# Attention sums divided untransposed by groups of eight heads, score maxima made further ahead

## The chip, the cores and the metric

One core of a Trainium2 chip runs the whole program. The metric is the device time of one execution in microseconds (us); lower is better.

## The reference, cut to what matters

A block of a transformer in float32: cross and self attention with 16 heads of 16 channels, then a mixture of experts.

```python
# x: (4, 512, 256), ctx: (4, 1601, 128)
def block(x, ctx):
    h = layernorm(x)
    q, k, v = heads(h @ Wq + bq), heads(h @ Wk + bk), heads(h @ Wv + bv)
    y = softmax(causal(q @ k.T * 0.25)) @ v
    qc, kc, vc = heads(h @ Wcq + bcq), heads(ctx @ Wck + bck), heads(ctx @ Wcv + bcv)
    y = y + softmax(qc @ kc.T * 0.25) @ vc
    x = x + tanh(g[0]) * (merge(y) @ Wp + bp)
    h = layernorm(x)
    return x + tanh(g[1]) * (shared_expert(h) + top2_of_7_experts(h))
```

## The kernel before, in words

There are 64 units of attention (4 sequences by 16 heads), called heads here. The program has three stages. The first prepares the queries, keys and values of all heads; it splits them into three bfloat16 parts and stores them in the device memory (`q_parts`, `k_parts`). The second is a loop over heads. The third projects the attention's result, normalizes again, and runs the shared expert, the router and the routed experts.

**The loop over heads.** A softmax needs the maximum of each query's scores before the exponentials. TensorE therefore makes the scores twice: first untransposed in 16 *pieces* a head (`MAX_PIECES`: twelve of 512 columns for the cross scores, then `tail`, `pair`, `self2`, `self3`), which VectorE reduces to maxima (`reduce_bank`, L1242); then transposed, in eight *groups* (`GROUPS`), with the maxima subtracted through two more rows of the operands. ScalarE takes the exponential of each group (L993), GpSimd masks the diagonal tiles (L1144), and TensorE multiplies them with the values in four phases (`values`, L669). The values have a column of ones, so that a phase also gives the sum of the exponentials.

**The maxima run ahead.** In the step of head u, the pieces c = 0 to 7 are the last eight of head u+1, and c = 8 to 15 are the first eight of head u+2 (`HALF` = 8, `reduce_piece`, `max_piece`). After its piece c = 7 VectorE joins the maxima in three small operations (`max_parts`, L1254, L1257, L1260). TensorE then transposes the result (`max_rows`, L592) after c = 11, ScalarE copies it out (L953), and a transfer on SyncE's queue puts it in its rows (`rows_load`, L471), for which the first scores of the next head wait.

**The order on TensorE is written out** by `schedule`: for each group g the piece 2g, the scores of g, the piece 2g+1, and then for odd g something more: the last phase of values of the head before (g = 1), the first phase and `norm` (g = 3), `rows` and the second phase (g = 5), the third phase (g = 7). Each engine runs its own instructions in order and waits on semaphores.

**The three banks.** The sixteen pieces, `norm` and `rows` (`ENTRIES`, 18 of them) take three PSUM banks in turn (`bank_of`, `RING` = 3). An entry may start when the entry three places before it in this order has been read out (`bank_free`):

```python
at = ENTRIES.index(item)
before = ENTRIES[at - RING]
```

**The division.** After the last phase ScalarE copies the sums of the head before (`sums_out`, L974), 128 rows by 512 queries. TensorE transposes them in four products (`norm`, L718), ScalarE copies the result (`norm_out`, L982), GpSimd adds the three cross parts (`cross_sums`, L1133, L1135), VectorE takes the reciprocals (L1326), and GpSimd multiplies and adds (`head_output`, L1125, L1128).

**After the loop** TensorE turns the attention's output back, 32 transposes with a copy by ScalarE for every four (L540, L1015), and projects it tile by tile (`project`, 16 tiles, L760). VectorE adds each tile to x (L1382) and normalizes it (`tail_stats`, `tail_scale`). `turn_xn(0)` transposes the first normalized sequence before the last four tiles, and the shared expert follows (`shared_up`, L786; ScalarE's `shared_silu`, L1032; VectorE's `shared_hidden`, L1352).

Of the kernel before, what the change touches and what calls it, by code (L numbers as in the profile page):

```python
# [17 lines left out]
NB = 4  # L18
# [74 lines left out]
HALF = NMAX // 2  # L93
MAXED = NMAX + HALF
# [4 lines left out]
def schedule():  # L99

    out = []
    for g in range(NG):
# [15 lines left out]
ENTRIES = [item for item in PE_ORDER if item[0] in ("max", "norm", "rows")]  # L118
# [6 lines left out]
RSUM_AT = HALF + 4  # L125

def run_steps(eng, step):

    step(0, 0, False, True, True)  # L130
    step(1, 1, True, True, True)
    heads = NR
    turns = (NU - 2 - 2) // heads
    with eng.Fori(0, turns) as i:
        for h in range(heads):
            step(i * heads + (h + 2), (h + 2) % NR, True, True, True)
    for u in range(heads * turns + 2, NU):
        step(u, u % NR, True, u + 1 < NU, u + 2 < NU)
# [13 lines left out]
def program(nc, a):  # L152
    ctx = ExitStack()
    with ctx:
# [10 lines left out]

        xn_rows = nc.dram_tensor("xn_rows", (NTOK, C), F32, kind="Internal").ap()
# [7 lines left out]
        xnT = sb("xnT", [P, 2, B * T])  # L174
# [42 lines left out]
        last_at = place["wq"][0]  # L217
        assert last_at + KSIZE + QSIZE <= place["wv"][0]
        kst = [region("kst")[:, r * KSIZE:(r + 1) * KSIZE] for r in range(NR - 1)]
        qst = [region("qst")[:, r * QSIZE:(r + 1) * QSIZE] for r in range(NR - 1)]  # L220
        kst.append(arena[:, last_at:last_at + KSIZE])
        qst.append(arena[:, last_at + KSIZE:last_at + KSIZE + QSIZE])
# [9 lines left out]
        rsum = sb("rsum", [P, TT, 2])  # L232
        yb = sb("yb", [P, TT, 2, D])

        router = sb("router", [P, 4 * NT * E8])
        sums = router[:, 0:TT * 4 * (D + 1)].rearrange("p (t q d) -> p t q d", t=TT, q=4)
        lg, key, s1, s2 = [router[:, NT * E8 * i:NT * E8 * (i + 1)].rearrange("p (t e) -> p t e", t=NT)
                        for i in range(4)]
        wr_cols = yb.rearrange("p a b d -> p (a b d)")[:, 0:2 * VW].rearrange("p (k w) -> p k w", k=2)
# [15 lines left out]
        def rt(*shape):  # L255
# [7 lines left out]
            if len(shape) == 3:  # L263
# [47 lines left out]
                 "m_all m_hi m_split rows_tr rows_evac rows_ready masked o_evac norm_mm norm_evac sums_half sums_in rsum_ready y_parts y_done  dve_chain "  # L311
                 "pool_chain y_turned y_freed proj_mm xn_turned xn_freed x2_ready tanh_done bias_gated x_biased wr_ready logits_mm logits_out logits_turned gap_ready exp2_done "
# [88 lines left out]
        def res_slot(s):  # L401
# [4 lines left out]
            return xnT[:, s % NS - NB, b * T:(b + 1) * T]  # L406
# [32 lines left out]
        def _(sp):  # L439
# [28 lines left out]
            def rows_load(v, r):  # L468

                sp.wait_ge(S["rows_evac"], v + 1)  # L470
# [39 lines left out]
            for v in range(NU - 2, NU):  # L510
                rows_load(v, v % NR)
# [1105 lines left out]
```

## Time and profile before

| what | value |
|---|---|
| median of 3 runs | 1414.95 us (1414.21 to 1415.78) |
| the profiled execution | 1413.27 us, of which the span from its first to its last instruction is 1411.5 us |
| TensorE busy | 1368.6 us, 97% of the span |
| VectorE, ScalarE, GpSimd busy | 880.9, 727.3, 365.4 us |
| preparation, loop over heads, the rest | up to 132.6 us, to 922.8 us, to the end |

The profile counts a matrix product as busy from its start to the end of its drain, so that two products that follow each other overlap; short waits hide in that overlap and have to be read from the starts in the timeline.

### The profile page before, as it was taken

To read this page: it belongs to the slowest core of one execution; us is meant where nothing else is said; L and a number is where in the kernel's file an instruction comes from. 1 tells how busy PE (TensorE), PEld (TensorE's weight loads), DVE (VectorE), ACT (ScalarE), POOL (GpSimd) and SP (SyncE) were. 2 spreads that over 40 slices of the span, in tenths; PEclk is the share of its full clock that TensorE was granted. 3 is DMA by queue.
4 is the path that set the end of the run, shared out by engine and by line. 5 is a ranking of instruction groups with operands and counts; after the bars stand their busy time and mean duration, and the time that the engine had idled before them with its cause. 6 is when DMAs were issued, how large, how long until landed. Compare 5 with 4: busy or idle time off the path is not lost.

```text
span 1411.5 us, 27301 instructions
## 1 busy us (share of the span) xinstructions
PE 1368.6 (97%) x7688; PEld 694.0 (49%) x7689; DVE 880.9 (62%) x1804; ACT 727.3 (52%) x1107; POOL 365.4 (26%) x743
## 2 busy tenths in 40 slices
PE   7988999999999999999999999989999999999997
PEld 4544333333333333333333333364556777777775
DVE  6776888888888888888888888653532222222221
ACT  4644667677777676767676767732210222222221
POOL 5655222222222222222222222200001232233232
PEclk9999999999999999999999999999999999999999
DMA  8754111111111111111111111057004122112111
GB/s 246 237 186 154 43 53 51 48 50 48 47 49 50 51 50 50 49 48 48 48 51 51 50 49 50 7 218 297 0 1 134 26 33 34 30 30 37 30 30 23
DMA packets 57711, 98.43 MB, mean 70 GB/s; under 512 B 7441, under 2 KB 42001, under 8 KB 56657
## 3 DMA queue, kind: packets, MB, share of 16 engines
q1 hardware_dynamic: 50384, 88.10, 18.8%
q0 software_dynamic: 7296, 9.97, 4.5%
q8 instruction: 15, 0.25, 0.1%
q14 instruction: 16, 0.12, 0.0%
HBM read 69.20 MB, written 28.58 MB: 69 GB/s over the span
## 4 chain that ended last, share of the span: by engine, by line
PE 88%; DMA 2%; DVE 2%; ACT 1%; issue 1%; POOL 1%; SPq 0%; POOLq 0%; ACTq 0%; DVEq 0%
PE ps L669 19%; PE ps L834 13%; PE ps L651 13%; PE ps L551 13%; PE ps L847 7%; PE ps L786 5%; PE ps L797 3%; PE ps L718 3%; PE ps L654 2%; PE ps L565 2%; PE ps L858 2%; DMA k_parts<-work 2%; PE ps L555 1%; PE ps L592 1%; PE ps L625 1%
## 5 line engine op out<-in xcount | busy, mean ns | idle before, releaser
L1242 DVE TENSOR_REDUCE mx<-ps 128x1 f32<-128x512 f32 (+1 forms) x832 | 515.1, 662 | 99.6 <-PE ps L551 69.3
L993 ACT ACTIVATE arena<-ps 128x1024 f32<-128x1024 f32 (+1 forms) x512 | 484.3, 995 | 138.7 <-PE ps L651 135.2
L669 PE MATMUL ps<-arena 128*32 128x512 f32 (+5 forms) x2432 | 290.9, 525 | 0.6 <-ACT arena L993 0.4
L551 PE MATMUL ps<-arena 96*128 96x512 bf16 x768 | 263.0, 382 | 7.3 <-DMA arena<-k_parts 2.9
L651 PE MATMUL ps<-arena 98*128 98x512 bf16 x832 | 264.4, 381 | 5.0 <-DMA arena<-rowst 4.9
L1144 POOL TENSOR_SCALAR_AFFINE_SELECT arena<-arena 128x128 f32<-128x128 f32 x256 | 74.8, 292 | 439.2 <-ACT arena L993 429.3
L834 PE MATMUL ps<-arena,work 128*128 x608 | 186.4, 460 | 0.6 <-issue 0.6
L551 PEld LDWEIGHTS ps<-arena 96*128 96x128 bf16 x768 | 74.1, 96 | 178.0 <-DVE mx L1242 103.2
L1520 DVE TENSOR_TENSOR work<-work,ps 128x352 f32<-128x352 f32 x76 | 39.6, 521 | 179.1 <-ACT work L1061 179.1
L834 PEld LDWEIGHTS ps<-arena,work 128*128 128x128 f32 x608 | 112.5, 190 | 57.4 <-issue 1.1
L1242 DVE TENSOR_REDUCE mneg<-ps 128x2 f32<-128x512 f32 (+2 forms) x192 | 112.4, 640 | 23.9 <-PE ps L561 23.4
L1061 ACT ACTIVATE work<-ps 128x352 f32<-128x352 f32 x76 | 35.2, 463 | 164.6 <-PE ps L834 164.6
L1186 POOL DMA_INDIRECT out<-bv,slot_table x38 | 59.9, 1575 | 207.3 <-DVE bv L1526 197.5
L669 PEld LDWEIGHTS ps<-arena 128*32 128x32 f32 (+1 forms) x2432 | 56.6, 108 | 113.1 <-issue 110.5
L651 PEld LDWEIGHTS ps<-arena 98*128 98x128 bf16 x832 | 76.5, 98 | 66.2 <-DMA arena<-rowst 6.1
L847 PE MATMUL ps<-arena,work 128*128 (+1 forms) x456 | 105.0, 379 | 0.8 <-ACT work L1067 0.8
L847 PEld LDWEIGHTS ps<-arena,work 128*128 128x128 f32 (+1 forms) x456 | 83.6, 190 | 11.4 <-issue 1.1
L1176 POOL DMA_INDIRECT wp<-xn_rows,slot_table x38 | 37.7, 993 | 173.5 <-DVE slot_table L1509 137.7
L1066 ACT ACTIVATE work<-ps 128x256 f32<-128x256 f32 x76 | 29.0, 382 | 99.7 <-PE ps L858 99.6
L786 PE MATMUL ps<-xnT,arena 128*128 128x512 f32 x176 | 77.1, 595 | 0.4 <-DVE work L1352 0.4
L654 PE MATMUL ps<-arena 98*128 98x512 bf16 (+3 forms) x256 | 66.1, 299 | 0.0
L1526 DVE TENSOR_SCALAR bv<-ps,router 128x256 f32<-128x256 f32 x38 | 18.4, 484 | 64.1 <-PE ps L847 64.1
(161 smaller groups left out, 1406.8 us busy)
## 6 DMA issues: line engine op xcount, KB each, us to landing
arena<-in_experts SPq DMA_DIRECT2D x8, 2176.0 KB, 12.2
arena<-k_parts SPq DMA_DIRECT2D x64, 198.1 KB
arena<-k_parts SPq DMA_DIRECT2D x64, 132.1 KB
arena<-q_parts SPq DMA_DIRECT2D x64, 96.0 KB
k_parts<-work SPq DMA_DIRECT2D x16, 300.0 KB, 5.2
q_parts<-work SPq DMA_DIRECT2D x12, 384.0 KB, 5.4
arena<-k_parts SPq DMA_DIRECT2D x64, 66.0 KB
arena<-q_parts SPq DMA_DIRECT2D x64, 64.0 KB
```

Of the source, the lines that this page charges most:

```text
L551: mm = pe.matmul(out, qx[:, qt * P:(qt + 1) * P], ks[0:KROWS, T + j * CHUNK:T + (j + 1) * CHUNK], start=True, stop=True)
L651: mm = pe.matmul(bk[:, 0:w], kst[r][0:KROWS + MROWS, T + kt * P:T + (kt + 1) * P], qst[r][0:KROWS + MROWS, 1, :], start=True, stop=True)
L654: mm = pe.matmul(bk[:, o0:o0 + w], kst[r][0:KROWS + MROWS, kt * P:(kt + 1) * P], qst[r][0:KROWS + MROWS, 0, kt * P:T], start=True, stop=True)
L669: mm = pe.matmul(ps[32 * q:32 * q + VW, 6, b0:b1], vst[0:kn, r % VR, TT + kt if cross else kt, :], pr[0:kn, c0:c0 + b1 - b0], start=(phase ...
L718: mm = pe.transpose(out[:, t * P:(t + 1) * P], osb[:, t * P:(t + 1) * P], ident[:, :])
L786: mm = pe.matmul(ps[:, 2 * (k0 % 2) + j, :], wgus[:, k, w0:w0 + P], xnT[:, k, tb * T:(tb + 1) * T], start=(k == 0), stop=(k == 1))
L834: mm = pe.matmul(ps[:, 2 * c + j, 0:CH], xgT[:, b, k, :], weights[:, bass.ds(e, 1), o:o + CH], start=(k == 0), stop=(k == 1))
L847: mm = pe.matmul(ps[:, 4, 0:C], hidT[0:m, it, :], weights[0:m, bass.ds(e, 1), o:o + C], start=(it == 0), stop=(it == IT - 1))
L993: act.activation(pr[:, c0:c0 + n], ps[:, 2 * (g % 2):2 * (g % 2) + 2, :].rearrange("p b n -> p (b n)")[:, 0:n], ACT.Exp, scale=SCALE).then ...
L1144: pool.affine_select(out=exps, in_=exps, pattern=[[1, P]], compare_op=ALU.is_ge, fill=0.0, base=0, channel_multiplier=-1).then_inc(S["mask ...
L1186: pool.indirect_dma_start(out=a["out"], out_offset=bass.IndirectOffsetOnAxis(slot_table[:, i, 1:2], 0), in_=yt[:, i % 2, :], in_offset=Non ...
L1242: return dve.tensor_reduce(m, out, AX_X, ALU.max)
```

## The change

- The division isn't transposed any more. Each head's sums are stored in the device memory (`o_parts`). For a group of eight heads they are loaded back so that 128 partitions are eight heads by 16 channels, the form that the projection reads. The denominators are loaded with their queries spread over partitions, summed by GpSimd and inverted by VectorE, stored and loaded again as broadcast rows; GpSimd sums, multiplies and adds tiles of 128x512. These steps are spread over the heads h = 2 to 7 of the next group.
- `norm` becomes the entry `spare`, which runs nothing, and `norm_out` is gone. `rows` moves from g = 5 to g = 3, ahead of the first phase of values. `HALF` = 8 becomes `BACK` = 5: c = 0 to 4 are the last five pieces of head u+1, and 27 pieces instead of 24 are made in the preparation.
- The transfer of the maxima's rows is issued by ScalarE, behind a wait for its own copy.
- The fourth operand buffer lies in `shared`; the shared expert's weights are loaded four heads before the end of the loop.
- After the loop there are no transposes of the output. The projection of sequences 2 and 3 is mixed with the first products of the shared expert, and the last group's division runs meanwhile. The loads of the routed experts come after the stores of the normalized rows.

```diff
-HALF = NMAX // 2
-MAXED = NMAX + HALF
+BACK = 5
+DONE = NMAX - BACK
+MAXED = NMAX + DONE
...
         if g == 3:
-            out += [("values", 0), ("norm",)]
+            out += [("rows",), ("values", 0)]
         if g == 5:
-            out += [("rows",), ("values", 1)]
+            out += [("spare",), ("values", 1)]
...
             def bank_free(u, *item):
                 at = ENTRIES.index(item)
-                before = ENTRIES[at - RING]
-                step = u if at >= RING else u - 1
+                at -= RING if ENTRIES[at - RING][0] != "spare" else 2 * RING
+                before = ENTRIES[at]
+                step = u if at >= 0 else u - 1
...
-                v, piece = (u + 1, c + HALF) if c < HALF else (u + 2, c - HALF)
+                v, piece = (u + 1, c + DONE) if c < BACK else (u + 2, c - BACK)
                 reduce_bank(v, piece, bank_of("max", c)).then_inc(S["max_red"], 1)
...
                 for c in range(NMAX):
-                    if (c < HALF and nxt) or (c >= HALF and nxt2):
+                    if (c < BACK and nxt) or (c >= BACK and nxt2):
                         reduce_piece(u, c)
-                    if nxt and c == HALF - 1:
+                    if nxt and c == BACK - 1:
                         for i in range(3):
                             max_parts(u + 1, i)
-                    if prev and c == RSUM_AT:
-                        reciprocals(u)
+                    if h == RECIP_IN and c == RECIP_AT:
+                        reciprocals(group)
...
                 act.activation(rowst[:, :], out[0:MROWS * 2 * TT, 0:P], ACT.Copy).then_inc(S["rows_evac"], 1)
+                act.wait_ge(S["rows_evac"], v + 1)
+                act.dma_start(qst[r][KROWS:KROWS + MROWS, :, :].rearrange("p i t -> p (i t)"), rowst[:, :]
+                              ).then_inc(S["rows_ready"], 16)
...
+            def head(u, j=None, h=None, loads=True):
+                sp.wait_ge(S["qk_done"], u * NG + NG)
+                if loads:
+                    stack_loads(u + NR, (BEGUN + h if j is not None else u) % NR)
+                if h == 2:
+                    den_load(j)
+                    num_load(j, 0)
+                if h == 3:
+                    num_load(j, 1)
+                if h == 4:
+                    num_load(j, 2)
+                    num_load(j, 3)
+                if h == 5:
+                    recip_load(j)
+                sums_store(u)
+                if h == 3:
+                    recip_store(j)
...
-            for b in range(B):
-                if b == B - 1:
-                    turn_xn(0)
-                project(b)
+            project(0)
+            project(1)
+            turn_xn(0)
             pe.wait_ge(S["shared_load"], 16)
-            shared_up(0)
+            shared_up(0, 0, 1)
+            project(2)
+            shared_up(0, 1, 2)
+            project(3)
+            shared_up(0, 2, IT)
...
             deviations(2 + B, 1, 2)
             xn_out(0)
+            shared_silu(0, 0, 1)
             deviations(3 + B, 2, 3)
+            shared_silu(0, 1, 2)
             deviations(4 + B, 3, 4)
-            shared_silu(0)
+            shared_silu(0, 2, IT)
...
-            shared_hidden(0)
+            second_norm(0, 2 * TT)
+            shared_hidden(0, 0, 1)
+            second_norm(2 * TT, 3 * TT)
+            shared_hidden(0, 1, 2)
+            second_norm(3 * TT, NT)
+            shared_hidden(0, 2, IT)
```

On VectorE `second_norm` runs the same operations per tile as before (`residual`, `tail_stats`, `tail_scale`), with the last group's reciprocals after tile 5. On ScalarE the store of the first normalized sequence stands ahead of `deviations(2 + B)` and behind a wait for the scaled rows.

## Rows read from the trace of the kernel before

**Rows 1.** The page, its first part: busy time, share, instructions.
```profile
PE 1368.6 (97%) x7688; PEld 694.0 (49%) x7689; DVE 880.9 (62%) x1804; ACT 727.3 (52%) x1107; POOL 365.4 (26%) x743
```
**Rows 2.** Windows: stretch, length, busy PE, PEld, DVE, ACT, POOL, clock, DMA share, GB/s.
```profile
400.00:800.00 400.00, 398.90 (x2743) 153.48 (x2737) 335.96 (x652) 283.34 (x360) 95.83 (x294) 1.00 0.15 50
```
**Rows 3.** Timeline of PE, one head: start, length (us), engine, line, what, count.
```profile
888.84 0.39 PE L551 MATMUL ps<-arena 96*128 96x512 bf16 x1
...
891.96 0.30 PE L555 MATMUL ps<-arena 96*128 96x65 bf16 x4
...
893.83 1.07 PE L669 MATMUL ps<-arena 128*32 128x512 f32 x8
894.83 0.66 PE L718 MATMUL ps<-ident,work 128*128 128x128 f32 x4
895.32 0.38 PE L551 MATMUL ps<-arena 96*128 96x512 bf16 x1
...
896.79 0.38 PE L551 MATMUL ps<-arena 96*128 96x512 bf16 x1
897.22 0.22 PE L592 MATMUL ps<-identb,mparts 128*16 128x128 bf16 x1
897.33 1.06 PE L669 MATMUL ps<-arena 128*32 128x512 f32 x8
...
899.85 0.38 PE L551 MATMUL ps<-arena 96*128 96x512 bf16 x1
900.16 1.06 PE L669 MATMUL ps<-arena 128*32 128x512 f32 x8
901.15 0.39 PE L551 MATMUL ps<-arena 96*128 96x512 bf16 x1
```
**Rows 4.** Timeline of DVE in the same head.
```profile
893.06 1.75 DVE L1242 TENSOR_REDUCE mneg<-ps 128x2 f32<-128x512 f32 x3 [0.34 <-PE ps L561]
894.85 0.17 DVE L1254 TENSOR_REDUCE mneg<-mx 128x4 f32<-128x16 f32 x1
...
895.26 0.17 DVE L1260 SCALAR_TENSOR_TENSOR mparts<-mneg,mparts 128x8 bf16<-128x8 f32 x1
895.74 2.54 DVE L1242 TENSOR_REDUCE mx<-ps 128x1 f32<-128x512 f32 x4 [0.31 <-PE ps L551]
```
**Rows 5.** Timeline of ACT in that head; of SP, an issue.
```profile
896.17 1.83 ACT L993 ACTIVATE arena<-ps 128x1024 f32<-128x1024 f32 x2 [0.26 <-PE ps L651]
897.89 0.25 ACT L953 ACTIVATE rowst<-ps 16x128 bf16<-16x128 f32 x1
...
505.11 0.68 SPq L471 DMA_DIRECT2D arena<-rowst  x1
```
**Rows 6.** Timeline where the loop starts: PE, ACT, SP.
```profile
132.59 0.39 PE L551 MATMUL ps<-arena 96*128 96x512 bf16 x1 [1.89 <-DVE arena L1315]
137.54 1.03 PE L651 MATMUL ps<-arena 98*128 98x512 bf16 x2 [4.56 <-DMA arena<-rowst]
...
138.67 1.28 ACT L993 ACT_TABLE_LOAD   x1 [6.41 <-PE ps L651]
139.97 1.94 ACT L993 ACTIVATE arena<-ps 128x1024 f32<-128x1024 f32 x2
...
128.40 2.93 SPq L490 DMA_DIRECT2D k_parts<-arena  x2
```
**Rows 7.** Timeline behind the loop: PE, DVE.
```profile
921.51 1.35 PE L669 MATMUL ps<-arena 128*32 128x512 f32 x14 [0.42 <-ACT arena L993]
...
932.03 10.87 PE L760 MATMUL ps<-wp,xnT 128*128 128x256 f32 x48
...
970.10 3.60 PE L786 MATMUL ps<-xnT,arena 128*128 128x512 f32 x8
...
933.18 0.48 DVE L1382 SCALAR_TENSOR_TENSOR x<-ps,tg,x 128x256 f32<-128x256 f32 x1 [6.01 <-PE ps L760]
...
942.57 0.40 DVE L1224 TENSOR_SCALAR shared<-x,mv,rs 128x256 f32<-128x256 f32 x1
```

More of the change, by code:

```diff
@@ L117 @@
 PE_ORDER = schedule()
-ENTRIES = [item for item in PE_ORDER if item[0] in ("max", "norm", "rows")]
+ENTRIES = [item for item in PE_ORDER if item[0] in ("max", "spare", "rows")]
 RING = 3
@@ L124 @@
 SCALE_LAG = 5
-RSUM_AT = HALF + 4
-def run_steps(eng, step):
[L130 to L137, printed above, removed]
+GH = P // D
+NGRP = NU // GH
+BEGUN = GH - 2
+TURNS = NGRP - 1
+DENS_IN, RECIP_IN, SUMS_IN, OUT_IN, RECIP_AT = 3, 4, 6, 7, 3
+assert GH % NR == 0 and BEGUN >= 2
+def run_steps(eng, step):
+    for u in range(BEGUN):
+        step(u, u % NR, u > 0, True, True)
+    with eng.Fori(0, TURNS) as i:
+        for h in range(GH):
+            step(i * GH + (BEGUN + h), (BEGUN + h) % NR, True, True, True, i, h)
+    for u in range(GH * TURNS + BEGUN, NU):
         step(u, u % NR, True, u + 1 < NU, u + 2 < NU)
@@ new lines, in _ @@
+            for u in range(BEGUN):
+                head(u)
+            with sp.Fori(0, TURNS - 1) as i:
+                for h in range(GH):
+                    head(i * GH + (BEGUN + h), i, h)
+            for h in range(GH):
+                u = (TURNS - 1) * GH + BEGUN + h
+                head(u, TURNS - 1, h, u + NR < NU)
+                if u == NU - NR:
+                    sp.dma_start(weights[:, SHARED, :], a["experts"][SHARED]).then_inc(S["shared_load"], 16)
+            den_load(NGRP - 1, 0, GH - 2)
@@ L577, in bank_free @@
                         pe.wait_ge(S["max_red"], min(n, NU * NMAX - MAXED) if isinstance(n, int) else n)
-                elif before[0] == "norm" and not (isinstance(u, int) and u == 0):
-                    pe.wait_ge(S["norm_evac"], step)
                 elif before[0] == "rows":
@@ L723, in _ @@
             values(NU - 1, (NU - 1) % NR, NPH - 1)
-            norm(NU)
             def logits():
@@ L973, in sums_out, with step @@
                 act.wait_ge(S["pv_done"], u * NPH)
+                if not (isinstance(u, int) and u == 1):
+                    act.wait_ge(S["o_written"], u * 16 - 16)
                 act.activation(osb[:, :], ps[:, 6, :], ACT.Copy).then_inc(S["o_evac"], 1)
[L976 to L984 removed]
+            def step(u, r, prev, nxt, nxt2, group=None, h=None):
                 for g in range(NG):
@@ L1378, in tail_scale, with residual @@
                 scale_rows(t)
-            for t in range(NT):
+            def residual(t):
                 dve.wait_ge(S["proj_mm"], t + 1)
```

265 lines of the change are left out of this document (146 added, 119 removed).

## The prediction

> **What bounds the kernel now.** I read the page first: TensorE is busy 97% of the span, VectorE 62%, ScalarE 52% [rows 1]. Then the windows of the loop over heads: in 400 us TensorE is busy 398.9, VectorE 336, ScalarE 283 [rows 2], at a granted clock of 1.00 (2.4 GHz). So the loop goes at TensorE's pace, and work taken from TensorE should be gained in full, unless a wait takes its place. VectorE, at 84%, is the engine to watch. Third, the timeline of one head, by starts, since the overlap of products hides short waits [rows 3]. A head takes 901.15 - 888.84 = 12.31 us. Fourth, the two ends of the loop [rows 6, 7].
>
> **What is removed.** The four transposes of `norm` take 895.32 - 894.83 = 0.49 us a head [rows 3]. The small waits around `rows` can be seen too: from the 512-column piece at 896.79 to the values at 897.33 are 0.54 us, where the same pair of steps without `rows` takes 900.16 - 899.85 = 0.31 [rows 3]. When `rows` leaves that place, 0.23 us go: the product itself (0.11) and its wait for a bank. Naively a head would take 12.31 - 0.49 - 0.23 + 0.11 = 11.70 us, and 61 full heads 37 us less.
>
> **Where a new wait comes.** `rows` now stands at g = 3, at index 8 of the ring, and needs the bank of entry 5, which is the piece c = 5. `BACK` = 5 puts the three operations of `max_parts` on VectorE between the reductions of c = 4 and c = 5. The piece c = 4 is the first product after the last values phase, so that VectorE has run dry by then. I count from that restart of TensorE, t0, in the trace 891.96 [rows 3].
> - TensorE, without a wait: the pieces from c = 4 to c = 7 have the same columns as before within 4 of some 2,200, so the values phase could start at +1.87 (893.83 - 891.96 [rows 3]), and `rows`, 0.11 long, goes ahead of it at about +1.75.
> - VectorE: c = 4 is `self3`, a product of 512 columns and one of 128. The second starts at +0.22, is 0.22 long like L592 [rows 3], and a reduction starts 0.04 behind a product's end (895.32 + 0.38 against 895.74 [rows 3, 4]). So its reduction starts at +0.48. A 512-wide one takes 0.69 with 0.62 between starts (four in 2.54 [rows 4]); it ends at +1.16. `max_parts` goes from 0.04 behind that (893.06 + 1.75 against 894.85) to 895.26 + 0.17, that is 0.62 behind it: +1.78 [rows 4]. The reduction of c = 5 starts at +1.71 to +1.78, since a start may overlap the last operation's end, and ends at +2.40 to +2.47.
> - TensorE's `rows` starts 0.17 behind that: in the old place the second of the four reductions ends at 895.74 + 0.62 + 0.69 = 897.05, and `rows` starts at 897.22 [rows 3, 4]. So it starts at +2.57 to +2.64, not +1.75, and the values at +2.68 to +2.75 instead of +1.87.
>
> Sum of a head: +0.81 to +0.88 for values that start late, -0.49 for the transposes, -0.23 around the old place of `rows`, and 0.04 that I allow for the changed order of the short pieces: **+0.13 to +0.20 us a head, I take 0.15**. Steps 1 to 61, 61 heads: **+9.2 us** (8 to 12). Behind the values phase VectorE is later than before, and I checked the ring on: the piece c = 11 needs the reduction of c = 8, which ends at +4.8, and comes at +5.15.
>
> **What lies beside other work.** In each step nothing on the other engines reaches TensorE's next need.
> - ScalarE loses `norm_out`, and copies the rows at about +2.83, 0.25 long, to +3.08 [rows 5]. Its new transfer has no row on this engine; SyncE's issue of the same transfer took 0.68 us [rows 5]. I take that: ScalarE is free at +3.8. The next exponential is wanted at +3.68 + 0.85 = +4.53 (896.17 - 895.32 is the 0.85 [rows 3, 5]). Cover 0.7 us; bounds 0.1 and 1.5 us for the issue, the upper price is a rival below.
> - SyncE gets per head one store of 256 KB, and per group four loads of denominators, four of numerators, two stores and two broadcast loads, each at 0.4 to 0.8 us of issue, as its present ones. With six stack loads that is at most some 9 us in a head of 12.4. Each load is wanted a head or more after its issue. The mean rate, 50 GB/s [rows 2], not quite doubles.
> - GpSimd does two to three 128x512 operations at the end of steps h = 6 and h = 7. I bound each by 0.3 and 1.6 us; the mask of the next head is wanted some 5 us later. If it were late, the values would be.
>
> **The start of the loop.** TensorE stands 4.56 us for the rows' transfer, which SyncE issues behind the last stores [rows 6]. ScalarE now issues it much earlier. What is late next: the exponentials, for ScalarE waits for the last `k_parts` store from the arena, whose issue begins near 130.8 [rows 6]. With a landing of 3.6 us, as these stores take, that is 134.5; then the table load of 1.28 us, and the first exponential starts near 136 instead of 139.97 [rows 6]. Less waiting at the low clock adds a little. I take -4.9 us (-3 to -6.5). The three further pieces in the preparation cost 0.22 us each on TensorE or 0.62 on VectorE, where nothing hides them: +1.0 (0.2 to 2). Together **-3.9**.
>
> **The last two heads** are at ScalarE's pace, without maxima of later heads. They lose one copy each: **-0.6** (0 to -1.5).
>
> **Behind the loop.** The last values end at 922.8. The first projection starts at 932.03, and the second sequence's products of the shared expert at 970.10 [rows 7]. So before it was 9.2 + 38.1 = 47.3 us, and in the 38.1 TensorE hardly waits. Now the projection starts at once, but `turn_xn(0)` comes after 8 tiles, at 8 x 0.906 = 7.25 us (10.87 / 12 [rows 7]). Its rows depend on VectorE: from the first residual to the scaling of the fourth tile are 942.57 - 933.18 = 9.4 us [rows 7]. One residual less and the reciprocals more, it is done at 1.15 + 9.25 + 0.4 = 10.8, and TensorE stands 3.7 us, then 1.1 more until ScalarE, which has a transfer to issue first, has copied. The last group's division needs three round trips of transfers, which I put at 17 us; it is wanted at 23. Two more waits of up to 1 us hang on ScalarE, which alternates between square root and Silu and so loads tables four times more, at 1.28 us each [rows 6]. In the sum 42 to 44 us instead of 47.3: **-4.3** (-2 to -6.5).
>
> In this trace a table load of 1.28 us is followed by its activation 0.02 us later [rows 6]. The Trainium skill (ScalarE: Activation LUTs, What ACT_TABLE_LOAD costs) gives 2.66 us for a switch, a drain of 1.38 included. By that rule the two switches on TensorE's path would cost 2.8 us more, an estimate from that page, and the tail would gain 1.5 us; I keep the row.
>
> **Sum.** +9.2 - 3.9 - 0.6 - 4.3 = +0.4 us on the profiled execution of 1413.3, that is 1413.7; its median of runs lies 1.7 us higher, so **1415.3 us**. About 0.2% (2.8 us) is what a measurement of this kernel can tell from no change.
>
> **The rivals.**
> - *The wait for the bank doesn't bind (faster).* If VectorE reduces c = 5 early, only `max_parts` remains: `rows` at +1.95, the values at +2.06, and a head is 0.19 - 0.49 - 0.23 + 0.04 = -0.49 us. 61 heads give -30, with the ends 1376 us. For it: the waits of today's ring are at most 0.2 us. Against it: VectorE's order in the code, and that the same wait shows at 897.22. Half of it gives 1395. Chance 0.18.
> - *ScalarE's own transfer holds the exponentials (slower).* Place: behind the copy of the rows, ahead of group 4. It decides from an issue, with the wait for its copy, of over 1.45 us; twice SyncE's 0.68 is 1.36. At 1.85 it would cost 0.4 us a head, +24, 1440 us. For it: the wait for its own copy has no row. Against it: the issue's row. Chance 0.10.
> - *The transfers come late (slower).* The broadcast loads and small rows fill the queue, and SyncE is late with the stacks or a store that ScalarE waits for. One late head in eight by 1.5 us is +12, 1427 us. Chance 0.06.
> - *The change doesn't bring its start and its tail.* The rows' transfer isn't what holds the start, since the stores are, and the tail waits eat its gain: +8, 1423 us. That lies in the forecast's own range.
>
> **How the numbers follow.** The forecast's mechanism has 0.66, with its own range from 1407 to 1424; within it I give 0.18 to a gain above 0.2%, 0.27 to neither, 0.21 to a loss, since the head's +0.15 may be off by 0.1 (6 us). With the rivals: faster 0.36, same 0.27, slower 0.37. The range reaches half way into the first rival and takes in the late transfers: 1396 to 1427; it leaves out the full first rival (about 0.10) and ScalarE's (0.10).
>
> **What would show it.** In the profile after, L592 starts about 0.8 us later than the piece before it would let it, with the reduction of c = 5 ending 0.17 us earlier; VectorE's three small operations stand between two 512-wide reductions; a head takes 12.4 to 12.5 us; the exponentials start near 136; TensorE idles some 4 to 5 us about 7 us behind the loop. It is wrong if a head takes under 12.2 or over 12.7 us, or if the release of L592 or L669 is ScalarE or a transfer.

## The result and the profile after

The changed kernel took 1432.48 us in the median of 4 runs (1429.79 to 1434.69); the kernel before took 1414.58 beside it (4 runs, 1412.98 to 1415.78). The ratio is 1.0126, with an interval from 1.0106 to 1.0147: **slower by 1.3%**, where 1415.3 was predicted and 1396 to 1427 was the range. The profiled execution took 1434.69 us, with a span of 1433.0.

The page's first part of the changed kernel, and its windows for the stretch of [rows 2], for the tail, and for a stretch of the shared expert:

```profile
PE 1347.3 (94%) x7400; PEld 664.3 (46%) x7401; DVE 881.6 (62%) x1748; ACT 709.4 (50%) x1039; POOL 332.8 (23%) x543
```
```profile
400.00:800.00 400.00, 373.23 (x2513) 132.78 (x2509) 323.28 (x602) 264.40 (x315) 74.34 (x184) 1.00 0.26 84
...
944.00:988.00 44.00, 38.06 (x133) 23.84 (x132) 26.22 (x79) 15.17 (x23) 6.79 (x7) 0.92 0.44 145
1068.00:1108.00 40.00, 37.98 (x147) 25.59 (x145) 7.12 (x17) 2.08 (x5) 3.10 (x3) 0.91 0.32 105
```

Against [rows 1] TensorE has 21 us less work, and in the loop it is busy 373.2 us of 400 instead of 398.9 [rows 2]: it lost work, and stands for some 27 us of these 400. The clock in the loop stayed at 1.00, so the clock has no part in it there.

Where the time went, by the starts of TensorE's steps in both profiled executions:

| stretch | before | after | difference | predicted |
|---|---|---|---|---|
| up to the start of step 1 | 151.94 | 147.13 | -4.8 | -3.9 |
| steps 1 to 61 | 749.21 | 774.59 | **+25.4** | +9.2 |
| steps 62, 63 | 21.64 | 20.63 | -1.0 | -0.6 |
| loop's end to the second sequence's shared products | 47.3 | 45.8 | -1.5 | -4.3 |
| the rest | 441.4 | 444.9 | +3.5 | 0 |

**One head.** The timeline of TensorE in the changed kernel, in the columns of [rows 3]; 504.23 is the restart t0 behind the last values phase, L663 is `max_rows`, L740 the values:

```profile
501.08 0.39 PE L623 MATMUL ps<-arena 96*128 96x512 bf16 x1
...
504.23 0.39 PE L637 MATMUL ps<-arena 96*128 96x512 bf16 x1
...
505.76 0.38 PE L623 MATMUL ps<-shared 96*128 96x512 bf16 x1
506.83 0.22 PE L663 MATMUL ps<-identb,mparts 128*16 128x128 bf16 x1 [0.69 <-DVE mx L1317]
507.05 1.06 PE L740 MATMUL ps<-arena 128*32 128x512 f32 x8
...
513.66 0.39 PE L623 MATMUL ps<-shared 96*128 96x512 bf16 x1
...
516.55 0.34 PE L637 MATMUL ps<-shared 96*128 96x384 bf16 x1 [1.18 <-DVE mx L1317]
```

VectorE in the same head and the next:

```profile
501.50 1.03 DVE L1317 TENSOR_REDUCE mx<-ps 128x1 f32<-128x512 f32 x2 [0.29 <-PE ps L623]
...
504.71 0.69 DVE L1317 TENSOR_REDUCE mneg<-ps 128x1 f32<-128x512 f32 x1 [1.10 <-PE ps L638]
505.44 0.17 DVE L1329 TENSOR_REDUCE mneg<-mx 128x4 f32<-128x16 f32 x1
...
506.01 1.89 DVE L1317 TENSOR_REDUCE mx<-ps 128x1 f32<-128x512 f32 x3
...
515.80 1.03 DVE L1317 TENSOR_REDUCE mx<-ps 128x1 f32<-128x512 f32 x2 [2.00 <-PE ps L633]
```

What is to be seen: the reduction of c = 4 starts at t0 + 0.48 and `max_rows` at t0 + 2.60, as the walk of the prediction had them, and `max_rows` is released by VectorE. A head takes 513.66 - 501.08 = 12.58 us. The second stand, at 516.55, was not foreseen. It comes once in eight heads, six times in the loop: such a head takes 13.90 to 14.14 us. In the VectorE rows it is a wait of 2.00 us ahead of the reduction at 515.80. In the head before, the same reduction, at 501.50, waits 0.29 us for its piece, an L623.
**ScalarE in that head:**

```profile
507.17 0.27 ACT L1009 ACTIVATE rowst<-ps 16x128 bf16<-16x128 f32 x1 [0.19 <-PE ps L663]
507.46 0.62 ACTq L1011 DMA_DIRECT2D arena<-rowst  x1
508.91 1.83 ACT L1046 ACTIVATE arena<-ps 128x1024 f32<-128x1024 f32 x2 [1.48 <-PE ps L722]
```

Its own transfer costs 0.62 us and is over 0.8 us before the next exponential, which waits for TensorE.

**The tail.** TensorE, then VectorE and GpSimd in the same stretch:

```profile
942.35 7.17 PE L815 MATMUL ps<-wp,xnT 128*128 128x256 f32 x32
954.69 1.97 PE L612 MATMUL ps<-ident,shared 128*128 128x128 f32 x8 [5.16 <-DVE shared L1299]
957.44 5.70 PE L839 MATMUL ps<-xnT,arena 128*128 128x512 f32 x8 [0.78 <-ACT xnT L1070]
962.97 3.62 PE L815 MATMUL ps<-wp,xnT 128*128 128x256 f32 x16
966.42 3.60 PE L839 MATMUL ps<-xnT,arena 128*128 128x512 f32 x8
```
```profile
948.24 1.14 DVE L1296 TENSOR_SCALAR sd<-mv 128x4 f32<-128x4 f32 x1
...
950.84 0.54 DVE L1399 RECIPROCAL work<-work 128x64 f32<-128x64 f32 x1
...
954.15 0.17 DVE L1296 TENSOR_SCALAR sd<-mv 128x4 f32<-128x4 f32 x1
```
```profile
948.09 1.27 POOL L1189 TENSOR_TENSOR xnT<-xnT,shared 128x512 f32<-128x512 f32 x1 [0.50 <-DMA work<-work]
949.50 1.26 POOL L1192 TENSOR_TENSOR xnT<-xnT,shared 128x512 f32<-128x512 f32 x1
```

TensorE stands 5.16 us for the fourth scaled tile, and after that stand the same eight products take 5.70 us instead of 3.60. The same small VectorE operation takes 0.17 us alone and 1.14 beside a GpSimd operation, where it ends 0.02 us behind that operation's end.

**The rest.** The row after, in the changed kernel, of the down products that begin the last part of the shared expert:

```profile
1093.34 9.32 PE L850 MATMUL ps<-arena,shared 128*128 128x256 f32 x24 [1.75 <-DVE x L1525]
```

In the kernel before the same 24 products, after the same wait of 1.75 us, took 6.03. They took 6.03 in all eleven later profiles, of changed kernels too. So this +3.3 us belongs to this one execution: the window around it has a granted clock of 0.91. It also accounts for the profiled execution lying 2.2 us above its median.

### The profile page after: what moved, and what is told of

Its sections match the earlier page's. It is cut to its first block, busy times and chain, and to the rows that moved or that the text cites. A ratio compares the mean times of both kernels' runs of the same rounds, so it can differ in the third digit from the quotient of the medians.

```text
span 1433.0 us, 26072 instructions
## 1 busy us (share of the span) xinstructions
PE 1347.3 (94%) x7400; PEld 664.3 (46%) x7401; DVE 881.6 (62%) x1748; ACT 709.4 (50%) x1039; POOL 332.8 (23%) x543
## 4 chain that ended last, share of the span: by engine, by line
PE 80%; DVE 9%; issue 3%; DMA 1%; ACT 1%; POOL 0%; DVEq 0%; POOLq 0%; SPq 0%; ACTq 0%
PE ps L740 19%; PE ps L887 13%; PE ps L623 10%; PE ps L722 10%; PE ps L900 7%; PE ps L839 5%; PE ps L850 4%; DVE mx L1317 3%; DVE mneg L1317 3%; PE ps L637 2%; PE ps L911 2%; PE ps L725 2%; PE ps L696 1%; PE ps L663 1%; PE ps L815 1%
## 5 line engine op out<-in xcount | busy, mean ns | idle before, releaser
L740 PE MATMUL ps<-arena 128*32 128x512 f32 (+5 forms) x2432 | 290.9, 525 | 1.4 <-ACT arena L1046 0.6
L623 PE MATMUL ps<-arena 96*128 96x512 bf16 x576 | 198.1, 382 | 4.4 <-DMA arena<-k_parts 2.5
L722 PE MATMUL ps<-arena 98*128 98x512 bf16 x624 | 197.9, 380 | 1.5 <-ACT arena L1046 1.4
L1317 DVE TENSOR_REDUCE mneg<-ps 128x2 f32<-128x512 f32 (+2 forms) x192 | 118.4, 642 | 63.0 <-PE ps L638 63.0
L623 PEld LDWEIGHTS ps<-arena 96*128 96x128 bf16 x576 | 55.6, 97 | 169.4 <-DVE mx L1317 116.6
L740 PEld LDWEIGHTS ps<-arena 128*32 128x32 f32 (+1 forms) x2432 | 56.7, 108 | 106.9 <-issue 98.6
L722 PEld LDWEIGHTS ps<-arena 98*128 98x128 bf16 x624 | 59.0, 98 | 50.3 <-ACT arena L1046 4.3
L722 PE MATMUL ps<-shared 98*128 98x512 bf16 x208 | 65.5, 379 | 0.0
L623 PE MATMUL ps<-shared 96*128 96x512 bf16 x192 | 65.5, 381 | 0.0
```

Source lines behind the costliest of these rows:

```text
L623: mm = pe.matmul(out, qx[:, qt * P:(qt + 1) * P], ks[0:KROWS, T + j * CHUNK:T + (j + 1) * CHUNK], start=True, stop=True)
L722: mm = pe.matmul(bk[:, 0:w], kst[r][0:KROWS + MROWS, T + kt * P:T + (kt + 1) * P], qst[r][0:KROWS + MROWS, 1, :], start=True, stop=True)
L740: mm = pe.matmul(ps[32 * q:32 * q + VW, 6, b0:b1], vst[0:kn, r % VR, TT + kt if cross else kt, :], pr[0:kn, c0:c0 + b1 - b0], start=(phase ...
L1317: return dve.tensor_reduce(m, out, AX_X, ALU.max)
```

## The experiments

Theories at the outset. **Main:** the loop is lengthened by a ring wait that the place of `max_parts` (`BACK` = 5) makes, 0.27 us a head, and by a stand of VectorE at its jump back. **Rivals:** the long loop bodies as such; the transfers; GpSimd's larger tiles, which fall in the same steps as the jump.

### Four pieces behind instead of five

```diff
-BACK = 5
+BACK = 4
```

> The changed kernel with BACK = 4, nothing else: the three operations of max_parts then run on VectorE during the last phase of values, one piece earlier. Theory (the rows' bank is held by the piece c = 5, whose reduction stands behind max_parts): L592's successor L663 starts at about +1.93 us from the restart of TensorE instead of +2.60, a head in the loop takes 11.8 to 11.95 us instead of 12.58, and the whole 40 to 46 us less than the changed kernel, 1387 to 1392 us. Rival (the new transfers and GpSimd's tiles slow the loop, the wait only shows it): a head stays above 12.4 us and the whole above 1425 us.

Measured: 1392.71 us (1391.13 to 1394.98), ratio 0.986 (0.9844 to 0.9877). The same places of one head, of TensorE and VectorE:

```profile
487.83 0.38 PE L623 MATMUL ps<-shared 96*128 96x512 bf16 x1
488.26 0.22 PE L663 MATMUL ps<-identb,mparts 128*16 128x128 bf16 x1
488.48 1.06 PE L740 MATMUL ps<-arena 128*32 128x512 f32 x8
```
```profile
486.04 0.17 DVE L1329 TENSOR_REDUCE mneg<-mx 128x4 f32<-128x16 f32 x1
...
486.79 2.54 DVE L1317 TENSOR_REDUCE mx<-ps 128x1 f32<-128x512 f32 x4 [0.17 <-PE ps L623]
```

`max_parts` now stands ahead of the piece c = 4, in time in which VectorE waits anyway, and TensorE's `rows` hardly waits any more: it comes 0.43 us after the piece instead of 1.07. A head takes 11.94 us, 0.64 less. So the wait was the whole difference between this kernel and one that is 1.4% faster than before. The heads at the jump still take 13.2 to 13.5 us.

### The rows at their old place

Eight pieces behind, and `rows` with ScalarE's copy at g = 5, so that the untransposed division stands almost alone:

```diff
-BACK = 5
+BACK = 8
-            out += [("rows",), ("values", 0)]
+            out += [("spare",), ("values", 0)]
-            out += [("spare",), ("values", 1)]
+            out += [("rows",), ("values", 1)]
```

> The changed kernel with BACK = 8 and the rows' entry back at g = 5 (spare at g = 3): only the new division, with ScalarE's transfer of the rows. Theory (the moved maxima cost, the division gains): a head takes 12.31 - 0.49 + 0.13 = 11.95 us, since the wait for the bank of c = 9 stays, the whole 36 to 42 us less than the changed kernel, 1391 to 1397 us. If the rows' transfer now lands too late for the next head's first scores, L722 waits for DMA arena<-rowst, and the head is 12.0 to 12.6 us. Rival (the division's transfers and GpSimd's tiles cost): above 1420 us with no such wait.

Measured: 1421.33 us (1420.05 to 1426.2), ratio 1.0065 (1.004 to 1.009). Many heads take 11.76 to 11.94 us, but almost a third take 12.8 to 14.1, among them the six at VectorE's jump with 13.3 to 13.5, and three, which are not at the jump, 15.5 to 15.7; the mean of steps 1 to 61 is 12.54. ScalarE's issue and TensorE's next use of the rows:

```profile
476.68 0.62 ACTq L1011 DMA_DIRECT2D arena<-rowst  x1
```
```profile
481.42 0.60 PE L722 MATMUL ps<-arena 98*128 98x512 bf16 x2 [1.27 <-DMA arena<-rowst]
...
494.39 0.60 PE L722 MATMUL ps<-arena 98*128 98x512 bf16 x2 [0.86 <-DMA arena<-rowst]
```

From the issue to the use are 4.7 us, for 4 KB. So the small transfer lands late here, while 256 KB transfers are under way, and TensorE waits for it 17 times, 21.3 us in all. These waits, the jumps and what follows them make 0.60 us a head over 11.94, more than the 0.49 of the saved transposes. That the large transfers make it late fits, but no run took them away. The second half of the change, the rows two groups sooner, is what the first half needs. It was the number of pieces that was chosen wrongly with it.

### Loop bodies of eight heads in the kernel before

```diff
-    heads = NR
+    heads = 2 * NR
```

> The kernel before with a loop body of eight heads instead of four on TensorE, VectorE, ScalarE and GpSimd; the work is the same. Theory (VectorE stands at the jump back because a body of eight heads has to be fetched again): VectorE stands some 2 us at each of the 7 jumps, TensorE 1.0 to 1.4 us, and the whole is 7 to 10 us slower than before, 1422 to 1425 us. Rival (GpSimd's three tiles of 128x512 at the end of the step h = 7 hold VectorE): no such stand, within 2 us of before.

Measured: 1412.10 us (10 runs, 1411.16 to 1414.1), ratio 0.9996 (0.9986 to 1.0006). No head takes more than 12.40 us. The DMA view shows no packet of the queue q14, instructions, between 300 and 800 us, where the changed kernel has 25:

```profile
q14 instruction: 25, 0.20, 0.1%
```

A body of eight heads alone is not what makes VectorE stand: from its branch to the next instruction are 0.3 us here and in the kernel before, against 2.8 to 3.0 in the changed kernel.

### VectorE's jump at another place of the head

VectorE's loop is turned, so that its body begins ahead of c = 4 of one step and ends there in another; GpSimd's tiles stay where they were.

```diff
-            run_steps(dve, step)
+            CUT = 4
...
+            step(BEGUN, BEGUN % NR, True, True, True, c1=CUT)
+            with dve.Fori(0, TURNS) as i:
+                for h in range(GH):
+                    step(i * GH + (BEGUN + h), (BEGUN + h) % NR, True, True, True, i, h, c0=CUT)
+                    step(i * GH + (BEGUN + h + 1), (BEGUN + h + 1) % NR, True, True, True, i, h + 1, c1=CUT)
```

> The changed kernel, with VectorE's jump back moved from ahead of the piece c = 0 to ahead of c = 4, where VectorE stands 1.1 us in each head anyway; the order of its work is the same. Theory (the jump's fetch): the step of 13.93 us in eight becomes 13.2 to 13.6, since 1.1 of some 2 us are covered but what is left delays the rows directly, and the whole is 2 to 5 us faster than the changed kernel. Rival (GpSimd's tiles): the stand of 2 us before the piece c = 0 stays where it is, and the time too.

Measured: 1438.28 us (1434.68 to 1440.08), ratio 1.0173 (1.015 to 1.0195). That the kernel would gain was a miss; where the stand is was not:

```profile
521.22 0.69 DVE L1317 TENSOR_REDUCE mneg<-ps 128x1 f32<-128x512 f32 x1 [2.63 <-PE ps L623]
```

The stand moved with the jump, from the pieces 14 and 15 to the piece c = 4, where TensorE has less work ahead of it to hide a stand; the six heads at the jump take 14.0 to 16.9 us. GpSimd's tiles are thereby out.

### VectorE's heads written out

```diff
-            run_steps(dve, step)
+            for u in range(NU):
+                j, h = divmod(u - BEGUN, GH) if BEGUN <= u < GH * TURNS + BEGUN else (None, None)
+                step(u, u % NR, u > 0, u + 1 < NU, u + 2 < NU, j, h)
```

> The changed kernel with VectorE's part of the 64 heads written out without a loop; the work and its order are the same, the other engines keep their loops. Theory (the stand of 2 us in every eighth head belongs to VectorE's own jump back): the steps of 13.9 us disappear, 7 x 1.35 = 9 us, and where VectorE waits on constants instead of registers the steps are 12.45 to 12.58, so 9 to 17 us less than the changed kernel, 1416 to 1424 us. Rival (another engine's jump or a transfer at that place holds VectorE): the stand stays and the time is within 3 us.

Measured: 1418.03 us (8 runs, 1416.31 to 1418.55), ratio 1.0031 (1.0021 to 1.0042), 14.5 us under the changed kernel. No long head is left, and the others take 12.50 instead of 12.58. The stands were 1.32 to 1.56 us over a normal head, six times, 8.4 us. The 0.08 a head is 4.5 us over the 56 heads of the loop. The third part, of 1.6 us, is within what runs differ by. The 0.08 shows between the piece c = 7 and the values, 1.20 us here and 1.29 in the changed kernel.

### TensorE's waits ahead of the rows

The values behind `rows` wait for the values' load (`v_ready`) and for ScalarE's last copy (`o_evac`). In the changed kernel they start 0.22 us behind `rows`, which itself needs 0.11. Both waits are put ahead of `rows`:

```diff
-                        if item[1] == 0:
-                            pe.wait_ge(S["v_ready"], u + 1)
-                            if prev:
-                                pe.wait_ge(S["o_evac"], u)
                         values(u, r, item[1])
-                    elif item[0] == "rows" and nxt:
+                    elif item[0] == "rows":
+                        pe.wait_ge(S["v_ready"], u + 1)
+                        if prev:
+                            pe.wait_ge(S["o_evac"], u)
+                        if not nxt:
+                            continue
```

> The changed kernel with TensorE's waits for v_ready and o_evac put ahead of the rows instead of behind them. Theory (behind a late L663 TensorE works off four waits before the values, which is why they start 0.22 us after it instead of 0.11): the values start 0.11 to 0.17 us after L663, a head takes 12.47 to 12.53 instead of 12.58 us, and the whole is 3 to 7 us faster than the changed kernel. Rival (the gap comes from the weights' load): no change.

Measured: 1425.63 us (1423.18 to 1427.0), ratio 1.0087 (1.007 to 1.0103), 6.9 under the changed kernel:

```profile
504.02 0.22 PE L663 MATMUL ps<-identb,mparts 128*16 128x128 bf16 x1 [0.70 <-DVE mx L1318]
504.13 1.07 PE L740 MATMUL ps<-arena 128*32 128x512 f32 x8
```

The distance is 0.11 now, and a head of the loop takes 12.48 us. Between `rows` and the values the trace of the changed kernel has two instructions that wait or compute registers, and this one has one: what had long been reached still costs 0.11 us behind an instruction that is late.

Steps 1 to 5 lie ahead of the loop and are written out in every version. There the same edit has the opposite effect: 12.53 us a head against 12.41 in the changed kernel. The changed kernel, then this one:

```profile
177.55 0.22 PE L663 MATMUL ps<-identb,mparts 128*16 128x128 bf16 x1 [0.53 <-DVE mx L1317]
177.76 1.06 PE L740 MATMUL ps<-arena 128*32 128x512 f32 x8
```
```profile
177.02 0.22 PE L663 MATMUL ps<-identb,mparts 128*16 128x128 bf16 x1 [0.74 <-DVE mx L1318]
177.14 1.07 PE L740 MATMUL ps<-arena 128*32 128x512 f32 x8
```

In both `rows` waits for VectorE's reduction. It starts 0.04 us behind VectorE's signal in the first and 0.25 in the second. So the edit helps in the loop and harms in written-out heads; "The same with the waits ahead" comes back to it.

### The first turn later in the tail

`turn_xn(0)` behind the twelfth tile instead of the eighth; ScalarE's and VectorE's orders go with it.

```diff
             project(0)
             project(1)
+            project(2)
             turn_xn(0)
             pe.wait_ge(S["shared_load"], 16)
-            shared_up(0, 0, 1)
-            project(2)
-            shared_up(0, 1, 2)
+            shared_up(0, 0, 2)
             project(3)
```

> The changed kernel with the third sequence's projection ahead of the first transposes of the normalized rows and of the shared expert. Theory (TensorE stands 5.2 us ahead of these transposes, and falls to the low clock): the 3.6 us of projection go into that stand and the products behind it run at 2.4 GHz, 4 to 7 us faster than the changed kernel. Rival (VectorE sets the pace there, which then only starts the shared expert later): within 2 us.

Measured: 1431.25 us (1430.02 to 1432.47), ratio 1.013 (1.0113 to 1.0146). That is within 2 us of the changed kernel, as the rival said; the theory expected more, and missed:

```profile
953.30 1.09 PE L612 MATMUL ps<-ident,shared 128*128 128x128 f32 x8
958.98 9.81 PE L839 MATMUL ps<-xnT,arena 128*128 128x512 f32 x16 [4.59 <-ACT xnT L1069]
```

The stand only changed its place, from ahead of the turn to behind it. ScalarE copies the turned tiles behind its square root, at 957.77, and that waits for VectorE. The whole tail takes 986.90 - 940.83 = 46.1 us, and took 45.8 in the changed kernel. So it is VectorE's and ScalarE's path, not TensorE's order, that sets it.

### Four pieces, heads written out

Four pieces behind, and the heads written out on TensorE, VectorE and ScalarE. GpSimd and SyncE keep their loops.

```diff
-BACK = 5
+BACK = 4
...
-    with eng.Fori(0, TURNS) as i:
+    if written_out:
+        for i in range(TURNS):
```

> The changed kernel with BACK = 4 and the heads written out on TensorE, VectorE and ScalarE. Theory: a head takes 11.85 us as in the written-out steps of the run with BACK = 4, with no stand at a jump, that is 61 x 0.09 + 7 x 1.4 = 15 us less than that run's 1393, 1375 to 1381 us, faster than both kernels. Rival (code that is never used twice has to be fetched all along and holds the engines): above 1390 us.

Measured: 1381.85 us (1381.17 to 1384.26), ratio 0.9781 (0.9765 to 0.9798): **the fastest version, 2.2% under the kernel before.** A head takes 11.85 us, and only one within the loop, of 12.38, and the last, of 12.93, are long. It lies 0.85 us above the range that was expected.

### The same with the waits ahead

```diff
+                        pe.wait_ge(S["v_ready"], u + 1)
+                        if prev:
+                            pe.wait_ge(S["o_evac"], u)
```

> The kernel after with four pieces in the last bank group (BACK 4), the heads written out on TensorE, VectorE and ScalarE, and TensorE's waits on v_ready and o_evac placed ahead of the rows. Theory (what is left of the wait for the maxima's rows still drains the queued waits behind it): in the four-piece version with the heads written out the rows' matmul and the values behind it still stand some 0.1 us apart; the waits put ahead give 0.05 to 0.11 us a head, 3 to 7 us: 1375 to 1379 us. Rival (with four pieces ahead the rows aren't late, so nothing drains and TensorE's pieces set the head): within 1 us of 1381.9.

Measured: 1388.61 us (5 runs, 1386.62 to 1389.63), ratio 0.9823 (0.981 to 0.9837): 6.8 us **slower** than without. Both the theory and its rival missed. This kernel's rows, then those of the version without:

```profile
511.61 0.38 PE L628 MATMUL ps<-arena 96*128 96x512 bf16 x1
512.16 0.22 PE L668 MATMUL ps<-identb,mparts 128*16 128x128 bf16 x1 [0.17 <-issue]
512.28 1.07 PE L745 MATMUL ps<-arena 128*32 128x512 f32 x8
```
```profile
507.87 0.38 PE L628 MATMUL ps<-arena 96*128 96x512 bf16 x1
508.22 0.22 PE L668 MATMUL ps<-identb,mparts 128*16 128x128 bf16 x1
508.43 1.06 PE L745 MATMUL ps<-arena 128*32 128x512 f32 x8
```

Ahead of `rows` the waits add 0.20 us, and behind it they give back 0.09; that 0.11 is the 0.12 by which a head is longer (11.97). It is also what the written-out steps 1 to 5 of the run with the waits ahead lose, 12.53 against 12.41. So the loss comes with the writing out, with five pieces as with four. A loop with four pieces and this edit was not run.

The trace's waiting instructions show how. In both four-piece versions VectorE's reduction is the last thing that `rows` needs. Without the edit the wait for it sits on the weight load of `rows` itself, which starts 0.04 us behind the reduction's signal (508.17, then 508.22). With the edit that wait stands first, at 511.94, and two further instructions with waits follow, at 512.05 and 512.13, before `rows` at 512.16, 0.25 us behind the signal. Inside a loop, where one wait needs a register computed, `rows` comes 0.12 us behind the signal with the edit and without. A wait that is long fulfilled costs some 0.1 us where it is worked off behind the late one, and the order in which the program has them is not that of the source.

### A longer body in the kernel before, and the changed body at another address

The first adds three copies of one column a head to VectorE in the eight-head version of before (24 instructions in a body). The second puts sixteen of them ahead of VectorE's loop in the changed kernel.

```diff
+                for k in range(3):
+                    dve.tensor_copy(pad[:, 3 * r + k:3 * r + k + 1], ident[:, k:k + 1])
```

> The kernel before with a loop body of eight heads, as in the earlier run, and three copies of one column a head more on VectorE (24 more instructions in the body). Theory of size (VectorE's jump stands some 2 us once the body is longer than what is held near the engine; the earlier eight-head body, 308 rows, was just within it): every eighth head 13.5 to 14 us instead of 12.3, instruction packets of queue 14 between 300 and 800 us, 1421 to 1427 us. Rival (something in the order of the changed kernel's body makes the stand, not its size): no long heads, no such packets, 1412 to 1415 us.

Measured: 1413.39 us (10 runs), ratio 1.0 (0.9991 to 1.001), no head over 12.40 and no packet of q14 between 300 and 800 us. The theory of size alone falls: this body has 354 VectorE instructions in the trace, those for registers and the branch included, and doesn't stand; that of the changed kernel has 316 and does.

```diff
+            for k in range(16):
+                dve.tensor_copy(pad[:, k:k + 1], ident[:, k:k + 1])
             run_steps(dve, step)
```

> The kernel after with sixteen copies of one column on VectorE ahead of its loop, so that the loop's body lies sixteen instructions later. Theory of size: the stand of about 2 us at each jump back stays, 1432 to 1435 us, long heads 13.8 to 14.2. Rival (where the body lies decides, not how long it is): the stands go, 1418 to 1423 us.

Measured: 1437.41 us (1437.33 to 1439.16), ratio 1.0171 (1.0156 to 1.0187). The stands stay, and are longer, with heads of 14.40 to 14.95 us and a first one of 16.51:

```profile
519.60 1.03 DVE L1318 TENSOR_REDUCE mx<-ps 128x1 f32<-128x512 f32 x2 [2.08 <-PE ps L634]
521.94 1.75 DVE L1318 TENSOR_REDUCE mneg<-ps 128x2 f32<-128x512 f32 x3 [1.31 <-issue]
```

A shift of sixteen instructions doesn't take them away. The second row is a new one: 1.31 us in which VectorE waited for nothing that the profile shows, 2.3 us behind the first reduction of the new turn. That the engine waits there for its instructions fits with it, and with the 25 packets of q14 in the changed kernel, 5 for each turn of the body; with VectorE written out there are 7 of them in that stretch, and no stand.

**Where the body lies was not tested by sixteen.** The traces of all runs say more than the two theories did. Place is counted here in VectorE's recorded instructions from the start of the program:

| kernel | body, its first and last | fetches within it, first turn | branch to the next instruction | q14 packets, 300 to 800 us |
|---|---|---|---|---|
| before | 337 to 503 | one | 0.3 us | 0 |
| before, eight heads | 337 to 667 | two | 0.3 us | 0 |
| the same, 24 more | 340 to 694 | two | 0.3 us | 0 |
| changed | 423 to 739 | three | 2.8 to 3.0 us | 25 |
| changed, 16 later | 439 to 755 | three | 2.8 to 3.0 us | 26 |
| changed, jump moved | 429 to 745 | three | 2.8 to 3.2 us | 26 |

The packets that go with VectorE have 8 KB. With VectorE written out one comes for every 126 to 133 of its instructions; the queue serves other engines too, but in the first turn of every looped kernel a packet comes near the instructions 450, 578 and 708, as far as its body reaches. A body that takes in three of these places is fetched anew in each turn: in the changed kernel a packet comes 1.0 us behind the branch at 512.86, and VectorE goes on 1.8 us after it. A body that takes in two is fetched once. So length and place decide together, as far as these programs tell, and the shift of sixteen left three places within the body. A shift by some 30 to 90 instructions, which would leave two, is the run that would prove it, and wasn't made.

## Why the prediction was wrong, point by point

1. **What bounds the kernel: right.** TensorE set the pace, and what it lost in work came back as a wait for VectorE.
2. **The walk to `rows`: right, step by step.** The reduction of c = 4 at +0.48, `rows` at +2.60 (2.57 to 2.64 was said), released by VectorE, and ScalarE's and SyncE's parts hidden. Taking the wait away by one piece gave 0.64 us a head. The rival "the wait for the bank doesn't bind", 0.49 under before, describes that kernel: 11.94 and 11.85 us against 12.31 - 0.49 = 11.82.
3. **The head's term, mis-sized: the first failed step.** +0.15 us was taken, +0.27 measured. The step in it is "the values at +2.68 to +2.75": they come at 507.05 - 504.23 = +2.82. The values were put one product's 0.11 us behind `rows`, as in the kernel before, where the second phase follows and needs neither `v_ready` nor `o_evac`; they stand 0.22 behind it. With 2.82 - 1.87 = +0.95 in place of +0.81 to +0.88 the prediction's own sum is 0.95 - 0.49 - 0.23 + 0.04 = +0.27. What the added 0.11 is was shown by the run with the waits ahead: semaphores passed behind a late instruction. Over the loop the mean head is 0.28 us longer, since the heads of before average 749.21 / 61 = 12.28 us: 17 us, where 9.2 were predicted.
4. **VectorE's jump: left out, the second failed step.** Nothing in the prediction prices the loop's jumps, although the body grew from four heads to eight. In the kernel before a jump takes VectorE 0.3 us and nothing shows of it; here it takes 2.8 to 3.0 us, as the body is fetched again. It costs 6 stands, 8.4 us, and with VectorE written out they are gone. With points 3 and 4, 17 + 8.4 = 25.4 us, the loop is accounted for.
5. **The start: right**, -4.8 for -3.9, by the mechanism that was named. The rows are there early, and the exponentials wait for the last `k_parts` store and the table load; the first starts at 136.13, where "near 136" was said:

```profile
134.84 1.28 ACT L1046 ACT_TABLE_LOAD   x1 [1.60 <-DMA k_parts<-arena]
```

6. **The tail: right in kind, a third in size.** Eight tiles took 7.17 us (7.25 was said). The stand at the turn was 5.16 us where 3.7 was said, since the fourth tile was scaled 12.3 us behind the loop and not 10.8. The VectorE rows show why: a small operation is some 1 us late beside GpSimd's 1.27 us tile, a neighbour that the prediction had bounded only by its own engine. The clock took 3.0 us more: the eight products behind the stand take 5.70 us, and 3.60 later, and the eight transposes ahead of them 1.97, against 1.09 in the run with the turn later; the granted clock of that window is 0.92, where the same window of before, with no stand in it, has 1.00. So TensorE was at 1.2 GHz for a part of it, behind a stand of 5.16 us. That the stand would be paid twice was not in the sum. The stand's 1.5 and the clock's 3.0 are more than the 2.8 us that were missed; the small gains against them were not taken apart. The late VectorE operation was not tested alone, but it comes again in the run with the turn later: 0.89 us instead of 0.17, and again it ends 0.03 us behind the GpSimd tile's end.
7. **The table loads: the trace decides.** ScalarE's switch to Silu in the tail, in the changed kernel:

```profile
961.86 1.28 ACT L1081 ACT_TABLE_LOAD   x1 [4.57 <-DMA xn_rows<-shared]
963.17 0.60 ACT L1081 ACTIVATE shared<-ps 128x512 f32<-128x512 f32 x1
963.78 1.28 ACT L984 ACT_TABLE_LOAD   x1
```

   The activation starts 0.03 us behind the load's end. The Trainium skill (ScalarE: Activation LUTs, What ACT_TABLE_LOAD costs) gives 2.66 us with its drain of 1.38. No row here shows such a drain: ahead of the first load ScalarE waited for a transfer, the second starts 0.02 us behind an activation's end, and TensorE waited for neither.
8. **The rivals.** ScalarE's own transfer: 0.62 us with 0.8 us to spare, refuted. Late transfers: none in the changed kernel, but 4.7 us from issue to use at the old place of `rows`, so the fear was of the right thing. The rival on the slow side should have been the jump.
9. **The rest** predicted 0, and the +3.3 us of this execution's clock stand in none of the eleven later profiles.

The median lay 5.5 us above the range. With the two failed steps at their measured size the prediction would have been 1415.3 + 7.8 (heads) + 8.4 (jumps) - 1.3 (start, last heads) + 2.8 (tail) = 1433.0, against 1432.48 measured. That sum closes because its terms are read from the same two traces; that they are two separate causes is shown by the runs with four pieces and with VectorE written out. Either of them alone would have brought it to 1423, still below the result. The head of 12.58 us stayed within the 12.2 to 12.7 that the prediction had set as its own test, so that test would not have found the error of the sum.

## What to carry to other kernels

When an operation is moved ahead on one engine, walk the other engine's order at the same place as closely: here one piece more or less ahead of three small VectorE operations was worth 0.64 us a head, 2.7% of the kernel, and the walk that predicted the wait to 0.03 us could have been used to choose the other number. Price what stands behind a stalled instruction too: the waits in its queue (0.11 us), and the clock behind a long stand (3.0 us). When a loop's body gets longer, look in the new trace at the first instruction behind the branch and at the packets of the instruction queue; if it stands there, write the engine's heads out.

## What the runs showed of the hardware that was not expected

- From the branch of VectorE's loop to its next instruction are 0.3 us in one program with a body of 354 instructions, and 2.8 to 3.2 in others with 316. Packets on the instruction queue go with it, 5 in a turn, and the place of the body among the places where packets are fetched separates the programs. A larger shift of the body would test it.
- Waits on semaphores reached long ago cost TensorE some 0.1 us each when they are worked off behind a late one. The same edit gained 6.9 us in a looped program and lost 6.8 us in one that is written out; in the second the late wait came to stand ahead of two others.
- A loop with waits on computed values is slower than the same heads written out with constants: 12.58 us with loops, 12.50 with VectorE written out, 12.41 in steps 1 to 5, where all engines are; with four pieces 11.94 against 11.85.
- A VectorE operation of 0.17 us took 1.14 and 0.89 beside a GpSimd tile of 1.27 and 1.26 us, both on data outside PSUM, and ended 0.02 to 0.03 us behind it both times.
- A transfer of 4 KB was used 4.7 us after its issue while 256 KB transfers were under way, though it had a queue of its own.
